# Second pass of an attention and gated linear attention block: halved products, a moved sparse product, a moved carry

## The chip, the cores and the metric

The kernel runs on one core of a Trainium2 chip. The metric is the device time of one execution in microseconds; the median of several executions counts.

## The reference, cut to what matters

The input is two sequences of 4096 tokens with 512 channels. Each goes through a linear attention with 16 heads (first block), and then through gated linear attention with 8 heads of 64 channels (second block). Around each block stand a layer norm, and a residual of another layer norm. The second block, in which the change lies:

```python
q1 = (x @ Wq) * scale; k1 = x @ Wk; v = x @ Wv
q2 = (x @ Wqa @ Wqb) * scale; k2 = softmax(x @ Wka @ Wkb)
gk1 = log_sigmoid(x @ Wg1a @ Wg1b + bg1) / 16
gk2 = log_sigmoid(x @ Wg2a @ Wg2b + bg2) / 16
e = softmax(x @ We); mask = one_hot(top_1(e)); rw = e * mask
o = gla(q1, k1, v, gk1) + sum over the 4 experts of gla(q2 * rw_e, k2 * rw_e, v, gk2 * mask_e)
g = x @ Wga @ Wgb
o = rmsnorm(o) * norm_w * silu(g);  out = o @ Wo
# gla: with G the running sum of gk in a chunk and S the state
#   o_t = (q_t exp(G_t)) S + sum over s <= t of (q_t exp(G_t) . k_s exp(-G_s)) v_s
#   S  <- exp(G_last) S + sum over s of (k_s exp(G_last - G_s)) v_s
```

The first `gla` is called dense here, the four others sparse: a token takes part in one expert alone.

## The kernel before, in words

A first pass over each sequence computes the sums of the linear attention. A second pass goes through the sequence in 32 tiles of 128 tokens, 64 tiles in all, and does the rest for a tile at a time. The change touches the second pass alone.

Five instruction queues run side by side, each in an order written out by hand, and wait for one another on semaphores: TensorE (`pe`), ScalarE (`act`), VectorE (`dve`), GpSimd (`pool`) and SyncE, which loads and stores. Each has a function `step(n, p)`. A step is spread over three tiles: the front of tile n, the back of tile m = n - 1, the tail of tile n - 2, and the first part (`ahead`) of tile n + 1. A queue never takes an instruction before the one that stands ahead of it.

TensorE's step: `low_rank` (the first halves of the low-rank products, bank 7), `route` (the four expert logits, bank 2), `project_v` (bank 1), `gates` (the second halves of gk1, gk2 and g, banks 4 to 6), `label_bc` (spreads each token's expert number over the rows, bank 7), `inter` and `intra` for tile m, then `project_k2`, `project_k`, `den`, `project_q1`, the tail's `og_transpose`, `project_q2`, `cumulate` (running sums of the gates), `out_mm`, `half_sums`, `y_mm`, `transposes`, `state_products`, `scores(n, 0)`, `xn_transpose` of tile n + 1, and `scores(n, 1)`. Matrices of 16 bits go as three products (line 310 to 312); f32 products take two matmul instructions each.

`inter` has two parts. The sparse part (line 481) multiplies the sparse queries with the states of all four experts, in 8 products whose contraction has 64 rows; it fills banks 0 to 3 and signals `ix_pe`. The dense part (line 489) multiplies the dense queries with the dense state, 4 products, into bank 7. `intra` (line 498) adds the scores within the tile times v to bank 7, 8 products.

VectorE's step: the masks of tile m's scores (`back_masks`, `back_carry1`, `back_masks2`), `front_router`, `front_low` (lines 1180 to 1183: the low halves of the low-rank products; `gates` waits for them), `front_label`, `back_carry` (line 1154: the new sparse states are added; the sparse part of `inter` waits for it, as it overwrites their banks), `front_onehot`, `front_masks` (lines 1215 and 1216), `back_select` (lines 1164 and 1167: from banks 0 to 3 each token takes its expert; `project_k2`, line 365, waits for it), `front_prob`, `front_logsig` (line 1222), `back_join`, the softmax of k2, `front_sil`, `back_norm`, qz of tile n + 1, the gated products, `back_normed` (line 1288), `back_gated` (line 1292), `back_out`, `front_decay`, `back_split` (lines 1112 and 1114), `ahead_residual` (line 1121: x1 of tile n + 1) and `ahead_low` (line 1125).

ScalarE's step: `front_low`, `front_label`, `front_v`, then the three passes over the gates (abs, line 729; exp, line 723; ln, line 725; all 1536 columns wide), `front_sig_high` (line 733, behind `front_logsig`), `back_square`, `front_ke`, `front_sig`, `ahead_z`, `back_og` (line 787: copies the transposed output, which `out_mm` needs), `front_exps` (lines 751 to 755), the norms, and the copies of the transposed q and k. The norm of x1 (`ahead_norm2`) is there too; it waits for line 1121. GpSimd adds the two score matrices (line 1018, `back_am`), builds `vm` (line 1025), and computes k2 (lines 1030 and 1034) and the decayed states (lines 1041 and 1042, behind `front_decay`).

Of the kernel before, what the change touches and what calls it, by code (L numbers as in the profile page):

```python
# [5 lines left out]
P = 128  # L28
# [5 lines left out]
H2, D2 = 8, 64  # L34
# [6 lines left out]
HALF = P // 2  # L41
# [24 lines left out]
def sandwich_kernel(nc, x_d, wqkv_d, wproj_d, bproj_d, wb_d, wl_d, ws_d, wo_d, nw_d, consts_d, out_d):  # L66
# [11 lines left out]
    with ExitStack() as ctx:  # L78
# [66 lines left out]
        v, vm = cut(2, C), cut(NEXP, C)  # L145
# [3 lines left out]
        q1T, k1T, q2T, k2T = cut(PAIRS, P), cut(PAIRS, P), cut(PAIRS, P), cut(PAIRS, P)  # L149
        assert cursor[0] <= REGION, cursor  # L150

        am1, am2 = cut(2, PAIRS, P, own=1), cut(2, PAIRS, P, own=1)
        sil, x1 = cut(2, C, own=1), cut(2, C, own=1)
        state0, statex = cut(PAIRS, P, own=1), cut(PAIRS, NEXP * D2, own=1)
# [46 lines left out]
        def S(name):  # L201
            if name not in sems:
                sems[name] = ctx.enter_context(nc.semaphore(name))
            return sems[name]
# [20 lines left out]
        def cur(n):  # L225
            return n + 2

        def prev(n):
            return n + 1
# [72 lines left out]
        def _(pe):  # L302
# [53 lines left out]

            def label_bc(n):
                pe.wait_ge(S("labi_ok"), cur(n))
                pe.wait_ge(S("low_ok"), cur(n))
                mm(bank[7][:, 2 * P:3 * P], ones16[:, :], lab_i[:, :], start=True, stop=True).then_inc(S("rx_pe"), 1)  # L360

            def second(out, which, k):
                if which == 1:
# [4 lines left out]
            def gates(n):  # L368
                pe.wait_ge(S("low_ok"), cur(n))
                pe.wait_ge(S("am1_ok"), prev(n))  # L370
                pe.wait_ge(S("am2_ok"), prev(n))
                for k, which in ((0, 1), (1, 1), (2, 0)):
                    last = second(bank[4 + k], which, k)
                last.then_inc(S("g_pe"), 1)
# [90 lines left out]

            by_row = bank[7].rearrange("p (f o r d) -> p f o r d", f=2, o=2, r=2)

            def inter(n, front):
                pe.wait_ge(S("state_ok"), cur(n))
                pe.wait_ge(S("q2T_ok"), cur(n))  # L470
                pe.wait_ge(S("am1_ok"), cur(n))
                pe.wait_ge(S("carry_ok"), cur(n))
                if front:
                    pe.wait_ge(S("ldiff_ok"), cur(n + 1))
                for half in (1, 0):
                    if half == 0 and front:
                        pe.wait_ge(S("v_ok"), cur(n + 1))
                    for r in range(2):
                        for odd in range(2):
                            h = slice(odd * D2, odd * D2 + D2)  # L480
                            last = mm(psum[:, 2 * half + odd, r * 256:r * 256 + 256], q2T[h, 2 * half + r, :],  # L481
                                      statex[h, 2 * half + r, :], start=True, stop=True)
                last.then_inc(S("ix_pe"), 1)
                if not front:
                    pe.wait_ge(S("out_ok"), n)
                if front:
                    pe.wait_ge(S("same_ok"), cur(n + 1))
                for pr in range(PAIRS):
                    last = mm(by_row[:, pr // 2, :, pr % 2, :], q1T[:, pr, :], state0[:, pr, :].rearrange("p (o d) -> p o d", o=2),
                              start=(pr == 0), stop=False, skip_group_check=True)  # L490
                last.then_inc(S("inter_pe"), 1)

            def intra(n, p):
                pe.wait_ge(S("am_ok"), cur(n))
                for pr in range(PAIRS):
                    for odd in range(2):
                        h = 2 * pr + odd
                        last = mm(by_row[:, pr // 2, odd, pr % 2, :], am1[:, odd, pr, :], v[:, p, h * D2:(h + 1) * D2],
                                  start=False, stop=True, skip_group_check=True)
                last.then_inc(S("o_pe"), 1)  # L500

            def og_transpose(n, back):
# [15 lines left out]
            def step(n, p, front=True, back=True, tail=True, ahead=True):  # L518
                m, mp, t = n - 1, 1 - p, n - 2
                if front:  # L520
                    low_rank(n)
                    route(n)
                    project_v(n)
                    gates(n)
                    label_bc(n)
                if back:
                    inter(m, front)
                    intra(m, mp)
                if front:
                    project_k2(n, back)  # L530
                    project_k(n, back)
                if ahead:
                    den(n + 1, mp, back=back)
                if front:
                    project_q1(n)
                if tail:
                    og_transpose(t, back)
                if front:
                    project_q2(n)
                    cumulate(n, back)  # L540
                if tail:
                    out_mm(t)
                if front:
                    half_sums(n)
                if ahead:
                    y_mm(n + 1)
                if front:
                    transposes(n)
                    state_products(n, p, ahead)
                    scores(n, 0)  # L550
                if ahead:
                    xn_transpose(n + 1, back)
                if front:
                    scores(n, 1)
# [526 lines left out]
        def _(dve):  # L1081
# [92 lines left out]
            def front_low(n):  # L1174
                dve.wait_ge(S("low1_ok"), cur(n))
                up, down = slice(0, LORA), slice(LORA, P)
                g, g_low, g_copy = slice(ROW_G, ROW_ONE), slice(0, 2 * GLR), slice(2 * GLR, 4 * GLR)
                parts = bank[7][:, 0:2 * P].rearrange("p (x c) -> p x c", x=2)
                minus = (ALU.mult, ALU.subtract)
                ve.scalar_tensor_tensor(low[down, 0:4:2, :], parts[up], LOW_SCALE, low[up, 0:4:2, :], *minus)  # L1180
                ve.scalar_tensor_tensor(low[g_low, 1, :], parts[g, 0, :], LOW_SCALE, low[g, 1, :], *minus)
                ve.tensor_scalar(low[g_copy, 1, :], parts[g, 0, :], LOW_SCALE, None, ALU.mult)
                ve.scalar_tensor_tensor(low[up, 3, :], parts[down, 1, :], LOW_SCALE, low[down, 3, :], *minus).then_inc(S("low_ok"), 1)
# [27 lines left out]
            def front_masks(n):  # L1211
                dve.wait_ge(S("rx_pe"), cur(n))
                dve.wait_ge(S("cum_pe"), prev(n))
                row = bank[7][:, 2 * P:3 * P]
                ve.scalar_tensor_tensor(same_d[:, :], row, lab[:, :], centred, ALU.is_equal, ALU.mult)
                ve.scalar_tensor_tensor(same_c[:, :], row, lab[:, :], causal, ALU.is_equal, ALU.mult).then_inc(S("same_ok"), 1)

# [87 lines left out]
            def step(n, p, front=True, back=True, tail=True, ahead=True):  # L1305
                m, mp, t = n - 1, 1 - p, n - 2
                if back:
                    back_masks(m)
                    back_carry1(m)
                    back_masks2(m)  # L1310
                if front:
                    front_router(n)
                    front_low(n)
                    front_label(n)
                if back:
                    back_carry(m)
                if front:
                    front_onehot(n, p)
                    front_masks(n)
                if back:  # L1320
                    back_select(m, mp)
                if front:
                    front_prob(n)
                    front_logsig(n)
                if back:
                    back_join(m)
                if front:
                    front_kmax(n)
                    front_kdiff(n)
                    front_lslow(n)  # L1330
                    front_kfac(n)
                    front_sil(n, p)
                if back:
                    back_norm(m)
                if ahead:
                    ahead_qz(n + 1, mp)
                    ahead_qz_split(n + 1)
                if front:
                    front_gated_1(n)
                    front_gated_q2(n)  # L1340
                if back:
                    back_normed(m)
                    back_gated(m, mp)
                if tail:
                    back_out(t, p)
                if front:
                    front_decay(n, p)
                if back:
                    back_split(m)
                if ahead:  # L1350
                    ahead_residual(n + 1, mp)
                    ahead_low(n + 1, mp)
# [151 lines left out]
```

## Time and profile before

| | |
|---|---|
| median of 3 runs | 2744.33 us (2741.7 to 2745.05) |
| span of the profiled execution | 2739.7 us, 55516 instructions |
| TensorE busy | 2579.3 us, 94% |
| VectorE busy | 1978.2 us, 72% |
| ScalarE busy | 1691.7 us, 62% |
| GpSimd busy | 958.6 us, 35% |

The profiler took one execution, and the page gives its span alone, from its first to its last instruction; no other time stands for that execution. Times in rows count from the start of the span. TensorE's matmuls overlap: where one starts, the one before has not ended, so the distance between two starts tells what a matmul costs in a row of them, and its own duration does not. PEld is TensorE's weight load. Line numbers are those of the kernel before.

### The profile page before, as it was taken

What the parts mean: (1) busy time and instruction counts of PE and PEld (TensorE: products, weight loads), DVE (VectorE), ACT (ScalarE), POOL (GpSimd) and SP (SyncE); (2) the same over time, 40 slices, a digit from 0 to 9 for tenths busy, and PEclk for the clock granted to TensorE, in tenths of its full rate; (3) what the DMA queues carried; (4) which work ended last, traced back from release to release, by engine and by line L of the source; (5) the groups of instructions that cost most, each with busy time, mean ns of one, the idle gap of its engine ahead of it and who ended that gap; (6) DMA issues with size and microseconds to landing.
All of it is one profiled execution on the core that took longest, in us unless ns stands there. A gap on an engine that the chain in (4) does not pass through costs nothing.

```text
span 2739.7 us, 55516 instructions
## 1 busy us (share of the span) xinstructions
PE 2579.3 (94%) x20208; PEld 1612.8 (59%) x20208; DVE 1978.2 (72%) x3750; ACT 1691.7 (62%) x3345; POOL 958.6 (35%) x750
## 2 busy tenths in 40 slices
PE   6999799999999999999869997999999999999997
PEld 3444466666666666666534444666666666666665
DVE  4443388888888888888644423888888888888886
ACT  4433367777777776767433434767677777676774
POOL 2795133333333333333222241333333333333332
PEclk9999899999999999999989998999999999999999
DMA  5121100000000000000022111000000000000000
GB/s 192 62 65 69 39 21 31 23 23 23 23 23 23 27 31 23 23 23 16 24 93 62 61 39 39 28 24 23 23 23 23 23 27 30 23 23 23 23 16 16
DMA packets 48388, 97.65 MB, mean 36 GB/s; under 512 B 5376, under 2 KB 5376, under 8 KB 47680
## 3 DMA queue, kind: packets, MB, share of 16 engines
q1 hardware_dynamic: 37008, 68.44, 7.6%
q10 hardware_dynamic: 9792, 17.83, 1.8%
q0 software_dynamic: 1520, 10.50, 1.0%
q8 instruction: 40, 0.66, 0.1%
q14 instruction: 28, 0.23, 0.0%
HBM read 63.19 MB, written 33.55 MB: 35 GB/s over the span
## 4 chain that ended last, share of the span: by engine, by line
PE 77%; DVE 14%; issue 5%; ACT 3%; DMA 0%; DVEq 0%; ACTq 0%; SPq 0%
PE psum L310 14%; PE psum L312 13%; PE psum L311 13%; PE psum L591 6%; DVE region L1167 5%; PE psum L445 5%; PE psum L481 5%; PE psum L462 4%; PE psum L435 4%; PE psum L321 2%; DVE region L1164 2%; DVE region L1154 2%; PE psum L454 1%; PE psum L365 1%; PE psum L339 1%
## 5 line engine op out<-in xcount | busy, mean ns | idle before, releaser
L310 PE MATMUL psum<-wb,region 128*128 128x512 f16 x768 | 292.0, 380 | 4.9 <-DVE region L1222 4.9
L311 PE MATMUL psum<-wb,region 128*128 128x512 f16 x768 | 292.0, 380 | 0.0
L312 PE MATMUL psum<-wb,region 128*128 128x512 f16 x768 | 291.9, 380 | 0.0
L1018 POOL TENSOR_TENSOR region<-region 128x1024 f32<-128x1024 f32 x64 | 150.2, 2346 | 373.7 <-DVE region L1139 373.7
L1030 POOL TENSOR_TENSOR region<-region,kfac 128x512 f32<-128x512 f32 x64 | 66.8, 1044 | 543.0 <-DVE kfac L1250 543.0
L1013 POOL TENSOR_TENSOR region<-region 128x1024 f32<-128x1024 f32 x64 | 146.5, 2289 | 289.1 <-DVE region L1373 231.1
L1025 POOL TENSOR_SCALAR region<-region,m 128x512 f32<-128x512 f32 x256 | 172.9, 696 | 181.2 <-DVE hm L1203 104.7
L1373 DVE SCALAR_TENSOR_TENSOR region<-psum,region 128x512 f16<-128x512 f32 x64 | 44.3, 692 | 262.2 <-ACT region L850 262.2
L733 ACT ACTIVATE region<-region 128x1024 f16<-128x1024 f32 x64 | 67.6, 1057 | 193.4 <-DVE region L1222 193.4
L591 PE MATMUL psum<-region 128*128 128x512 f16 x768 | 176.2, 379 | 0.0
L481 PE MATMUL psum<-region 64*128 64x256 f32 x1024 | 130.9, 394 | 26.8 <-DVE region L1154 26.8
L1042 POOL TENSOR_TENSOR region<-region,decay 128x1024 f32<-128x1024 f32 x64 | 149.6, 2338 | 0.0
L1034 POOL TENSOR_TENSOR region<-region 128x512 f32<-128x512 f32 x64 | 81.7, 1276 | 192.8 <-ACT region L755 192.8
L1167 DVE SCALAR_TENSOR_TENSOR region<-psum,m,region 128x512 f32<-128x512 f32 x192 | 144.1, 751 | 6.8
L445 PE MATMUL psum<-region 64*128 64x128 f32 x2048 | 148.2, 284 | 0.0
L1125 DVE SCALAR_TENSOR_TENSOR region<-region,rstd 128x512 f16<-128x512 f32 x64 | 48.1, 751 | 138.3 <-ACT region L684 138.3
L445 PEld LDWEIGHTS psum<-region 64*128 64x128 f32 x2048 | 124.1, 187 | 31.1 <-issue 24.6
L850 ACT ACTIVATE region<-psum 128x512 f16<-128x512 f32 x64 | 38.2, 597 | 164.7 <-PE psum L312 164.7
L667 ACT ACTIVATE region<-psum 128x512 f32<-128x512 f32 x256 | 137.5, 589 | 0.0
L481 PEld LDWEIGHTS psum<-region 64*128 64x128 f32 x1024 | 106.2, 190 | 46.2 <-issue 46.0
L1369 DVE TENSOR_TENSOR region<-region 128x512 f16<-128x512 f32 x64 | 95.7, 1496 | 49.8 <-ACT region L863 49.8
L659 ACT ACTIVATE junk<-psum 128x512 f32<-128x512 f32 x128 | 76.6, 599 | 85.9 <-PE psum L312 85.9
(235 smaller groups left out, 7638.4 us busy)
## 6 DMA issues: line engine op xcount, KB each, us to landing
region<-x_in SPq DMA_DIRECT2D x128, 256.0 KB, 2.6
q_cols<-region ACTq DMA_DIRECT2D x64, 256.0 KB, 2.4
region<-q_cols SPq DMA_DIRECT2D x64, 256.0 KB, 2.8
out_rows<-region SPq DMA_DIRECT2D x60, 256.0 KB, 2.0
region<-wb_in POOLq DMA_DIRECT2D x1, 3072.0 KB, 11.6
region<-wqkv_in SPq DMA_DIRECT2D x4, 512.0 KB, 5.8
region<-wqkv_in POOLq DMA_DIRECT2D x2, 1024.0 KB, 5.7
region<-wproj_in POOLq DMA_DIRECT2D x2, 1024.0 KB, 7.5
```

Of the source, the lines that this page charges most:

```text
L310: mm(out, lhs(0), rhs(0), start=start, stop=False)
L311: mm(out, lhs(0), rhs(1), start=False, stop=False)
L312: return mm(out, lhs(1), rhs(0), start=False, stop=stop)
L445: last = mm(bank[where[odd]][:, pr * P:(pr + 1) * P], kT[h, pr, :], qT[h, pr, :], start=True, stop=True)
L481: last = mm(psum[:, 2 * half + odd, r * 256:r * 256 + 256], q2T[h, 2 * half + r, :], statex[h, 2 * half + r, :], start=True, stop=True)
L591: last = mm(bank[4 + j], xn8[:, p * GT + t, x * C + j * P:x * C + (j + 1) * P], k16[:, y_, :], start=first and begins, stop=final and ends ...
L667: ac(dst.rearrange("p a b -> p (a b)"), bank[where], ACT.Copy).then_inc(S(done), 1)
L1013: nc.gpsimd.tensor_tensor(kacc, kacc, k16, ALU.add).then_inc(S("kacc_ok"), 1)
L1018: nc.gpsimd.tensor_tensor(am1[:, :, :, :], am1[:, :, :, :], am2[:, :, :, :], ALU.add).then_inc(S("am_ok"), 1)
L1025: last = nc.gpsimd.tensor_scalar(vm[:, e, :], v[:, p, :], m4[:, p, e:e + 1], 1.0, ALU.mult, ALU.mult)
L1042: nc.gpsimd.tensor_tensor(statex.rearrange("p a (e d) -> p a e d", e=NEXP), carryx.rearrange("p a (e d) -> p a e d", e=NEXP), decay[:, :, ...
L1167: ve.scalar_tensor_tensor(to, of[:, :, e, :], m4[:, p, e:e + 1], to, ALU.mult, ALU.add).then_inc(S("sel_ok"), 1)
```

## The change

Four things are changed. The dense part of `inter` and `intra` are split by output rows: each product of 128 columns of weights becomes two of 64, one for each half of the output's rows. `inter` falls into `inter_sparse` and `inter_dense`; on TensorE, `label_bc` and `inter_sparse` now stand ahead of `gates`, and `inter_dense` and `intra` behind it. The label is spread into bank 6 instead of bank 7, so `label_bc` waits for the masks of tile m (`am2_ok`) and `gates` waits until the label has been read (`same_ok`). On VectorE, `front_label` and `back_carry` stand ahead of `front_low`. 22 empty lines at the top of the file are taken out as well.

```diff
@@ -356,8 +334,8 @@
 
             def label_bc(n):
                 pe.wait_ge(S("labi_ok"), cur(n))
-                pe.wait_ge(S("low_ok"), cur(n))
-                mm(bank[7][:, 2 * P:3 * P], ones16[:, :], lab_i[:, :], start=True, stop=True).then_inc(S("rx_pe"), 1)
+                pe.wait_ge(S("am2_ok"), prev(n))
+                mm(bank[6][:, 0:P], ones16[:, :], lab_i[:, :], start=True, stop=True).then_inc(S("rx_pe"), 1)
 
             def second(out, which, k):
                 if which == 1:
@@ -368,7 +346,7 @@
             def gates(n):
                 pe.wait_ge(S("low_ok"), cur(n))
                 pe.wait_ge(S("am1_ok"), prev(n))
-                pe.wait_ge(S("am2_ok"), prev(n))
+                pe.wait_ge(S("same_ok"), cur(n))
                 for k, which in ((0, 1), (1, 1), (2, 0)):
                     last = second(bank[4 + k], which, k)
                 last.then_inc(S("g_pe"), 1)
@@ -465,7 +443,7 @@
 
             by_row = bank[7].rearrange("p (f o r d) -> p f o r d", f=2, o=2, r=2)
 
-            def inter(n, front):
+            def inter_sparse(n, front):
                 pe.wait_ge(S("state_ok"), cur(n))
                 pe.wait_ge(S("q2T_ok"), cur(n))
                 pe.wait_ge(S("am1_ok"), cur(n))
@@ -481,13 +459,15 @@
                             last = mm(psum[:, 2 * half + odd, r * 256:r * 256 + 256], q2T[h, 2 * half + r, :],
                                       statex[h, 2 * half + r, :], start=True, stop=True)
                 last.then_inc(S("ix_pe"), 1)
+
+            def inter_dense(n, front):
                 if not front:
                     pe.wait_ge(S("out_ok"), n)
-                if front:
-                    pe.wait_ge(S("same_ok"), cur(n + 1))
                 for pr in range(PAIRS):
-                    last = mm(by_row[:, pr // 2, :, pr % 2, :], q1T[:, pr, :], state0[:, pr, :].rearrange("p (o d) -> p o d", o=2),
-                              start=(pr == 0), stop=False, skip_group_check=True)
+                    for rows in (slice(0, HALF), slice(HALF, P)):
+                        last = mm(by_row[rows, pr // 2, :, pr % 2, :], q1T[:, pr, rows],
+                                  state0[:, pr, :].rearrange("p (o d) -> p o d", o=2),
+                                  start=(pr == 0), stop=False, skip_group_check=True)
                 last.then_inc(S("inter_pe"), 1)
 
             def intra(n, p):
@@ -495,8 +475,9 @@
                 for pr in range(PAIRS):
                     for odd in range(2):
                         h = 2 * pr + odd
-                        last = mm(by_row[:, pr // 2, odd, pr % 2, :], am1[:, odd, pr, :], v[:, p, h * D2:(h + 1) * D2],
-                                  start=False, stop=True, skip_group_check=True)
+                        for rows in (slice(0, HALF), slice(HALF, P)):
+                            last = mm(by_row[rows, pr // 2, odd, pr % 2, :], am1[:, odd, pr, rows], v[:, p, h * D2:(h + 1) * D2],
+                                      start=False, stop=True, skip_group_check=True)
                 last.then_inc(S("o_pe"), 1)
 
             def og_transpose(n, back):
@@ -521,10 +502,13 @@
                     low_rank(n)
                     route(n)
                     project_v(n)
+                    label_bc(n)
+                if back:
+                    inter_sparse(m, front)
+                if front:
                     gates(n)
-                    label_bc(n)
-                if back:
-                    inter(m, front)
+                if back:
+                    inter_dense(m, front)
                     intra(m, mp)
                 if front:
                     project_k2(n, back)
@@ -1211,7 +1195,7 @@
             def front_masks(n):
                 dve.wait_ge(S("rx_pe"), cur(n))
                 dve.wait_ge(S("cum_pe"), prev(n))
-                row = bank[7][:, 2 * P:3 * P]
+                row = bank[6][:, 0:P]
                 ve.scalar_tensor_tensor(same_d[:, :], row, lab[:, :], centred, ALU.is_equal, ALU.mult)
                 ve.scalar_tensor_tensor(same_c[:, :], row, lab[:, :], causal, ALU.is_equal, ALU.mult).then_inc(S("same_ok"), 1)
 
@@ -1310,11 +1294,11 @@
                     back_masks2(m)
                 if front:
                     front_router(n)
+                    front_label(n)
+                if back:
+                    back_carry(m)
+                if front:
                     front_low(n)
-                    front_label(n)
-                if back:
-                    back_carry(m)
-                if front:
                     front_onehot(n, p)
                     front_masks(n)
                 if back:
```

## Rows read from the trace of the kernel before

**Rows 1.** The page: busy time, share of the span, instructions of each engine.
```profile
PE 2579.3 (94%) x20208; PEld 1612.8 (59%) x20208; DVE 1978.2 (72%) x3750; ACT 1691.7 (62%) x3345; POOL 958.6 (35%) x750
```

**Rows 2.** Chain in order of time, one step: start us, us, what ran.
```profile
1002.78 0.76 DVE region L1164
...
1005.95 0.39 PE psum L365
...
1034.94 0.76 DVE region L1164
```

**Rows 3.** Waits, 700 to 1300 us: total us, times, longest.
```profile
DVE region L1164 <- PE psum L481: 29.0, 19, 1.6
...
PE psum L365 <- DVE region L1167: 9.2, 19, 0.5
...
PE psum L481 <- DVE region L1154: 5.9, 19, 0.4
...
DVE region L1121 <- ACT rstd L663: 4.5, 19, 0.3
```

**Rows 4.** Timeline, 994 to 1008 us: start, us, engine, line, count [idle before].
```profile
995.05 0.23 PE L310 MATMUL psum<-region,wl 128*128 128x128 f16 x1
...
997.22 0.21 DVE L1191 TENSOR_SCALAR ldiff<-psum,lmax 128x4 f32<-128x4 f32 x1
...
999.08 0.38 PE L312 MATMUL psum<-wb,region 128*128 128x512 f16 x1
...
999.10 1.29 DVE L1154 TENSOR_TENSOR region<-psum,region 128x512 f32<-128x512 f32 x2
...
999.94 0.38 PE L366 MATMUL psum<-ws,region 128*128 128x512 f16 x1
...
1000.36 1.45 ACT L729 ACTIVATE region<-psum 128x1536 f32<-128x1536 f32 x1 [0.23 <-PE psum L366]
...
1000.65 2.00 PE L481 MATMUL psum<-region 64*128 64x256 f32 x16 [0.27 <-DVE region L1154]
...
1000.91 0.34 DVE L1216 SCALAR_TENSOR_TENSOR same_c<-psum,lab,cst 128x128 f32<-128x128 f32 x1
...
1002.57 0.97 PEld L489 LDWEIGHTS psum<-region 128*128 128x128 f32 x8 [0.33 <-issue]
...
1003.40 1.48 ACT L725 ACTIVATE region<-region 128x1536 f32<-128x1536 f32 x1
...
1003.57 1.90 PE L498 MATMUL psum<-region 128*128 128x64 f32 x16
...
1006.11 1.76 DVE L1222 SCALAR_TENSOR_TENSOR region<-psum,region 128x1536 f32<-128x1536 f32 x1
```

**Rows 5.** Timeline, 1011 to 1025 us, of ScalarE, GpSimd, VectorE and TensorE.
```profile
1013.11 1.02 ACT L787 ACTIVATE ogT<-psum 128x1024 f16<-128x1024 f16 x1 [0.97 <-PE psum L509]
...
1016.25 1.27 POOL L1034 TENSOR_TENSOR region<-region 128x512 f32<-128x512 f32 x1 [3.10 <-ACT region L755]
...
1017.19 0.88 DVE L1288 TENSOR_TENSOR og<-region,ors 128x512 f32<-128x512 f32 x1
...
1019.63 1.16 POOL L1041 TENSOR_TENSOR region<-region,decay 128x512 f32<-128x512 f32 x1 [2.10 <-DVE decay L1267]
...
1021.54 0.75 DVE L1121 SCALAR_TENSOR_TENSOR region<-psum,rstd,region 128x512 f32<-128x512 f32 x1 [0.20 <-ACT rstd L663]
...
1021.84 0.69 PE L454 MATMUL psum<-region 128*64 128x64 f32 x16
...
1022.43 1.95 PE L462 MATMUL psum<-region 128*64 128x256 f32 x16
```

**Rows 6.** VectorE's groups by line and shape: total us, mean ns of one.
```profile
L1114 DVE TENSOR_TENSOR og<-og 128x512 f16<-128x512 f32 x64 | 89.4, 1397 | 2.2
...
L1288 DVE TENSOR_TENSOR og<-region,ors 128x512 f32<-128x512 f32 x64 | 55.6, 868 | 1.8 <-ACT ors L782 1.8
...
L1292 DVE TENSOR_TENSOR og<-og,region 128x512 f32<-128x512 f32 x64 | 44.3, 692 | 2.2
```

More of the change, by code:

```diff
@@ L523, in step @@
                     project_v(n)
-                    gates(n)
                     label_bc(n)
                 if back:
-                    inter(m, front)
+                    inter_sparse(m, front)
+                if front:
+                    gates(n)
+                if back:
+                    inter_dense(m, front)
                     intra(m, mp)
@@ L1312, in step @@
                     front_router(n)
-                    front_low(n)
                     front_label(n)
@@ L1317, in step @@
                 if front:
+                    front_low(n)
                     front_onehot(n, p)
```

## The prediction

> **What bounds the kernel now.** I read the page first: TensorE is busy 94% of the span, VectorE 72%, ScalarE 62% [rows 1]. The change touches only the second pass, a loop of 64 tiles. The chain in order of time gives its beat: the same selection instruction starts at 1002.78 and again at 1034.94, so a step lasts 32.16 us [rows 2]. So much for the average; what a moved instruction is worth depends on which queue is late where it stands. The waits between 700 and 1300 us [rows 3] show four, each 19 times in 19 steps: the sparse product L481 waits for the carry L1154 (5.9/19 = 0.31 us a step), the key projection L365 waits for the selection L1167 (0.48), the selection L1164 waits for L481 (1.53), and the residual L1121 waits for rstd (0.24). The reader is to see that TensorE loses about 0.8 us a step around the sparse product, and that VectorE, once the selection has begun, loses only that 0.24 until L1121. VectorE is in front of its work there; it is a second queue with almost no room.
>
> One step in detail [rows 4]. TensorE starts the low-rank product at 995.05, ends the v projection (last start 999.08), does the four gate matmuls (last start 999.94), the label, and at 1000.65 the sparse product. ScalarE takes the gates at 1000.36 (abs), then exp and ln; ln ends at 1003.40 + 1.48 = 1004.88. VectorE's log-sigmoid L1222 needs that ln, but starts only at 1006.11, when the selection is done: ln is 1.23 us early. From 1006.11 VectorE runs its fixed list to L1121, which starts at 1021.54 after an idle 0.20 [rows 5]. L1121 writes x1; from its start to the next low-rank product, one beat after 995.05 at 1027.21, it is 5.67 us of norm, transposes and copy, each waiting for the one before. So a step is a ring: low rank, gates or selection, L1222, VectorE's list, L1121, next low rank.
>
> **The change, part by part, for this step.**
> Carry ahead of the low-rank split: L1191 ends at 997.22 + 0.21 = 997.43; a maximum over four columns and L1154 (1.29) follow, so the carry is there at about 999.0 instead of 999.10 + 1.29 = 1000.39. The four split instructions move behind it; VectorE's list up to L1216 is the same work in another order, so the masks end as before at 1000.91 + 0.34 = 1001.25. The split's reader, the gates, comes after that anyway: no price.
>
> Label and sparse product ahead of the gates: TensorE is free of the v projection 0.22 after 999.08, at 999.30 (from there four matmuls of 512 columns start up to 999.94, 0.215 each). The label has a quarter of the columns, 0.06: 999.36. The carry is no longer waited for. The sparse product uses the array in two row halves; how long such a change of shape takes behind running matmuls stands in no single row. Below: nothing. Above: the weight loader's 0.33 us in front of L489, the change back. I take 0.10, nearer to nothing because the loader's wait lies partly beside the last products. Sparse at 999.46, 1.19 earlier than 1000.65. From L481's start to L489's is 1.92, the change back included: the gates start at 999.46 + 1.92 = 1001.38 (the masks, ended at 1001.25, release the label's bank in time, with 0.13 to spare). The last gate matmul starts 3 x 0.22 later, 1002.03, against 999.94: **the gates are 2.09 us later**.
>
> The Trainium skill (TensorEngine Tiling, Key Properties) says that switching the tiling mode drains the engine. The loader's 0.33 in front of L489 agrees with it; were the first change that long as well, the gates would come 0.23 later than I take, a case inside my range.
>
> Two column halves: 8 dense instructions become 16, and 16 intra-tile ones 32 (each f32 product is two). Intra before: from 1003.57, 16 in 1.90. After, the form is that of L454, 16 of which take 1022.43 - 1021.84 = 0.59 [rows 5], 0.037 each: 32 x 0.037 = 1.18. Dense, 128x64 with 128 columns, is in no row. Below: L454 (64 columns), 0.59. Above: L462 (256 columns), whose 16 are busy 1.95. I take the middle of the spacing by columns, 16 x 0.06 = 1.0, as much as before (1003.57 - 1002.57). So dense and intra end about 1002.03 + 0.22 + 0.1 + 1.0 + 1.18 = 1004.5, between 1004.1 and 1005.5. The selection ends first or last: it begins 2.13 after L481 (1002.78 - 1000.65), and L365 3.17 after that: 999.46 + 2.13 + 3.17 = 1004.76 for L365, against 1005.95. By these numbers TensorE is **1.19 us earlier** at the key projection.
>
> What is late next. ScalarE's abs moves with the gates: 1002.45, and ln ends at 1004.88 + 2.09 = 1006.97. VectorE is done with the selection at 1004.7 and must now wait for ln: L1222 starts at 1007.00, **0.89 later** than before, although everything on TensorE is earlier. Behind L1222 stand the join, the key softmax, the low half of the log-sigmoid, qz, the gated products, the output, the split and L1121, all in VectorE's order, and ScalarE's own list behind L1222's result. TensorE's 1.19 us goes where it meets these: a little at the q projection, which needs L1222, and the rest at the output product, which needs ScalarE's copy L787. That had 0.97 us of idle time in front of it [rows 5], so 0.89 later in its inputs leaves it at about 1013.1, where it was. TensorE is then on the old timetable, and waits again for x1 at L462, which stood right behind L1121's end before (21.54 + 0.75 = 22.29, L462 at 22.43).
>
> VectorE's list, then: +0.89 at L1222; -0.20 because L1121's wait for rstd is used up. One instruction gets shorter: L1288 takes 868 ns on average, L1292 of the same size 692 [rows 6]; L1288 starts at 1017.19 while GpSimd's L1034 runs from 1016.25 for 1.27 [rows 5]. L1034 waits for ScalarE's exponentials, which stand behind L787 and so stay where they were; L1288 comes 0.89 later, when L1034 is over: -0.18. The Trainium skill (SBUF, Who interferes with whom) has the rule: VectorE with two SBUF inputs and GpSimd take one port pair in turns. The rows of L1288 agree. Without that relief the sum would be 62 x 0.69 = 43 us.
>
> Sum: 0.89 - 0.20 - 0.18 = +0.51 us a step. The steps that hold both a tile and the tile before it are 31 a batch, 62 in all: 62 x 0.51 = **32 us**. First and last steps of a batch gain or lose below 1 us each. The profiled execution's span is 2739.7, and the median of the three timed runs 2744.33, 4.6 above; I add the sum to the median: **2776 us**.
>
> Bounds of the likeliest case: no drain and a full relief +0.41, less 0.1 for the rough starts of overlapped rows; a full drain and no relief +0.92. 62 times these: 2763 to 2802. The dense halves' bounds change nothing: up to 1005.5 instead of 1004.76 TensorE is still ahead of where L787 holds it.
>
> **Rivals.**
> (a) *The port pair gives more back (faster).* The split of the gated output, L1114 on og, takes 1397 ns, twice the 692 of L1292 [rows 6], while GpSimd's state product L1041, started at 1019.63 [rows 5], runs beside it. If the shifted list reached L1114 outside L1041, 0.70 us would go, more than the 0.51, and the step would be 0.19 shorter: -12, 2732. It decides once L1114 starts ahead of L1041 instead of behind it. Against it: what releases L1041 is VectorE's decay, just ahead of this split, so the two shift together.
> (b) *VectorE is not held by ln (faster).* If ScalarE's three passes ended early enough, selection and list would both be about 1.1 earlier, 62 x 1.1 = 68, 2676. For it: VectorE waits 1.53 a step for L481 today, and L1222 almost never for ln. Against it: 4.52 us from 1000.36 to 1004.88 are three full-width passes with no idle time to shorten; it turns when ln is less than 0.2 late instead of 0.89.
> (c) *It cancels.* Slack in the ring that the rows don't show (a ScalarE queue behind x1, TensorE at L462) takes most of the 0.51: within 5 us.
> (d) *The halves don't overlap.* At the old intra spacing of 0.11 (16 in 1.9, end included), 48 take 5.3 us; L365 comes at 1007.7, 1.75 later than before, and TensorE, with no wait left, carries it to L462: +108, 2852. Against it: L454's 0.037.
>
> **Chances.** Forecast 0.66, (a) 0.10, (b) 0.10, (c) 0.10, (d) 0.04. A change below 0.2% (5.5 us) can't be told from none. Faster: (a) and (b), 0.20; same: (c), 0.10; slower: the forecast and (d), 0.70. For 8 in 10 the range goes down to 2730, taking in (a), and up to 2805; outside lie (b), (d) and edges. The likeliest alone: 2763 to 2802.
>
> **What would show it.** In the profile after: a beat of about 32.7; L481 at some 4.4 us after the low-rank start instead of 5.6; VectorE's wait for L481 nearly gone, and in its place some 2 us a step in front of L1222, released by the ln L725; TensorE waiting for L787 at the output product and for L1121 at L462; L498's successors at 0.037 each; L1288 at 0.69. If L1222 shows no wait for ln, or the beat is under 32.1, the prediction is wrong; if the wait is there and the beat is not longer, VectorE's list had room that I did not see.

## The result and the profile after

The changed kernel takes 2772.12 us, median of 4 runs (2771.02 to 2773.53), against 2743.28 for the kernel before in the same rounds: a ratio of 1.0106, with a 95% interval of 1.0091 to 1.0120. It is 28.8 us slower; forecast were 2776 us, with a range of 2730 to 2805, and slower with a chance of 0.70. Its profiled execution has a span of 2770.1 us, 30.4 more than before.

Line numbers move by the deleted empty lines and the new ones. L1222 is now L1206, L1121 is L1105, L1288 is L1272, L1114 is L1098, L725 is L709, L787 is L771, L481 is L459, L365 is L343, L1164 is L1148, L462 is L440, L1112 is L1096, L1125 is L1109, and GpSimd's L1041 and L1042 are L1025 and L1026.

The chain of waits of the changed kernel in order of time, without the many matmuls of the projections (start us, us, what ran). It answers to [rows 2].

```profile
1007.38 0.23 PE psum L288
...
1011.84 1.93 PE psum L459 x16
1013.77 0.54 PE psum L342 x2
...
1014.77 1.46 ACT region L713
1016.23 0.18 ACT lexp L702 x2
1016.41 1.38 ACT region L707
1017.81 1.49 ACT region L709
...
1034.28 0.75 DVE region L1105
1035.03 0.14 issue
1035.17 1.95 PE psum L440 x16
...
1039.88 0.23 PE psum L288
```

This is the ring of the prediction in one piece: low rank, sparse product, gates, ScalarE's three passes, VectorE's list, x1, TensorE, next low rank. A turn is 1039.88 - 1007.38 = 32.50 us, against 32.16. The page's summary of the whole chain says the same: the first line is of the kernel before, the second of the changed kernel. TensorE's share falls from 77% to 51%, VectorE's and ScalarE's grow.

```profile
PE 77%; DVE 14%; issue 5%; ACT 3%; DMA 0%; DVEq 0%; ACTq 0%; SPq 0%
PE 51%; DVE 27%; ACT 12%; issue 9%; DVEq 0%; DMA 0%; SPq 0%; ACTq 0%
```

The same step in the timeline (start, us, engine, line, count, idle time before and what ended it), beside [rows 4, 5].

```profile
1011.77 2.00 PE L459 MATMUL psum<-region 64*128 64x256 f32 x16
...
1013.91 0.75 DVE L1148 TENSOR_SCALAR region<-psum,m 128x512 f32<-128x512 f32 x1 [0.44 <-PE psum L459]
...
1014.36 0.38 PE L344 MATMUL psum<-ws,region 128*128 128x512 f16 x1
...
1014.66 1.09 PE L468 MATMUL psum<-region 128*64 128x128 f32 x16
...
1015.59 1.10 PE L479 MATMUL psum<-region 128*64 128x64 f32 x32
...
1017.08 0.39 PE L343 MATMUL psum<-ws,region 128*128 128x512 f16 x1 [0.39 <-DVE region L1151]
...
1019.33 1.76 DVE L1206 SCALAR_TENSOR_TENSOR region<-psum,region 128x1536 f32<-128x1536 f32 x1 [2.05 <-ACT region L709]
```

Count from the low-rank start, 995.05 before and 1007.38 after. The sparse product comes at 4.39 instead of 5.60, the key projection L343 at 9.70 instead of 10.90. The gates' last matmul comes at 6.98 instead of 4.89, and L1206 at 11.95 instead of 11.06, after 2.05 us in which VectorE does nothing. TensorE is 1.2 us early, and gives it back further on, where it waits for ScalarE's copy and for x1:

```profile
1026.34 0.39 PE L288 MATMUL psum<-wo,ogT 128*128 128x512 f16 x1 [0.69 <-ACT ogT L771]
```

The waits between 700 and 1300 us (total, times, longest), answering to [rows 3]. VectorE's wait for the sparse product is down from 29.0 to 7.9, its wait for ln, which had no row before, is 36.8, and TensorE has two new ones.

```profile
DVE region L1206 <- ACT region L709: 36.8, 18, 2.0
...
PE psum L288 <- ACT ogT L771: 13.1, 19, 0.7
...
PE psum L440 <- DVE region L1105: 9.4, 19, 0.5
...
DVE region L1148 <- PE psum L459: 7.9, 18, 0.4
...
PE psum L343 <- DVE region L1151: 7.0, 18, 0.4
```

Where the 30.4 us are, by the starts of the selection L1148. Its 29 middle distances of a sequence are 32.50 instead of 32.16 or 32.17: 2 x 29 x 0.335 = 19.4. The first distance of each sequence is 34.86 and 34.84 instead of 31.05: 7.6. The last is 1.2 and 1.4 longer: 2.6. The first selection comes 1.1 later, which need not be the change's: over the eleven profiles of this case it lies anywhere between 358.8 and 363.9. Together 30.7; the way from the first sequence to the second and the end of the second make up the rest.

### The profile page after: what moved, and what is told of

Read it like the earlier page. It is cut to its first block, busy times and chain, and to the rows that moved or that the text cites. A ratio compares the mean times of both kernels' runs of the same rounds, so it can differ in the third digit from the quotient of the medians.

```text
span 2770.1 us, 58588 instructions
## 1 busy us (share of the span) xinstructions
PE 2557.9 (92%) x21744; PEld 1544.3 (56%) x21744; DVE 1965.7 (71%) x3750; ACT 1689.6 (61%) x3345; POOL 970.1 (35%) x750
## 4 chain that ended last, share of the span: by engine, by line
PE 51%; DVE 27%; ACT 12%; issue 9%; DVEq 0%; DMA 0%; SPq 0%; ACTq 0%
PE psum L288 9%; PE psum L289 8%; PE psum L290 8%; PE psum L575 6%; PE psum L423 5%; PE psum L459 5%; PE psum L440 4%; ACT region L709 3%; ACT region L713 3%; ACT region L707 3%; DVE region L1215 2%; DVE region L1256 2%; DVE region L1105 2%; DVE region L1287 2%; DVE region L1156 2%
## 5 line engine op out<-in xcount | busy, mean ns | idle before, releaser
L1002 POOL TENSOR_TENSOR region<-region 128x1024 f32<-128x1024 f32 x64 | 150.8, 2356 | 358.8 <-DVE region L1123 358.8
L1206 DVE SCALAR_TENSOR_TENSOR region<-psum,region 128x1536 f32<-128x1536 f32 x64 | 112.5, 1757 | 131.9 <-ACT region L709 131.9
L713 ACT ACTIVATE region<-psum 128x1536 f32<-128x1536 f32 x64 | 93.1, 1455 | 148.5 <-PE psum L344 148.5
L440 PE MATMUL psum<-region 128*64 128x256 f32 x1024 | 124.5, 383 | 28.9 <-DVE region L1105 28.9
L1026 POOL TENSOR_TENSOR region<-region,decay 128x1024 f32<-128x1024 f32 x64 | 149.5, 2336 | 0.0
L1109 DVE SCALAR_TENSOR_TENSOR region<-region,rstd 128x512 f16<-128x512 f32 x64 | 48.0, 751 | 134.9 <-ACT region L668 134.9
L423 PEld LDWEIGHTS psum<-region 64*128 64x128 f32 x2048 | 124.1, 187 | 31.0 <-issue 24.6
L288 PE MATMUL psum<-wo,ogT 128*128 128x512 f16 x256 | 99.7, 389 | 44.5 <-ACT ogT L771 44.5
L459 PE MATMUL psum<-region 64*128 64x256 f32 x1024 | 131.4, 397 | 7.7 <-DVE region L1138 7.7
```

Source lines behind the costliest of these rows:

```text
L288: mm(out, lhs(0), rhs(0), start=start, stop=False)
L423: last = mm(bank[where[odd]][:, pr * P:(pr + 1) * P], kT[h, pr, :], qT[h, pr, :], start=True, stop=True)
L440: last = mm(psum[odd * D2:odd * D2 + D2, 3 * (pr // 2), (pr % 2) * 256:(pr % 2) * 256 + 256], k2g[:, h * D2:(h + 1) * D2], vm[:, :, h * D2 ...
L713: ac(gch, psum[:, 4:7, :].rearrange("p a b -> p (a b)"), ACT.Abs).then_inc(S("abs_ok"), 1)
L1002: nc.gpsimd.tensor_tensor(am1[:, :, :, :], am1[:, :, :, :], am2[:, :, :, :], ALU.add).then_inc(S("am_ok"), 1)
L1026: nc.gpsimd.tensor_tensor(statex.rearrange("p a (e d) -> p a e d", e=NEXP), carryx.rearrange("p a (e d) -> p a e d", e=NEXP), decay[:, :, ...
```

## The experiments

The theory is that of the prediction. The rivals are that TensorE's new order or array shapes cost the time, and that time saved on TensorE counts wherever it is saved. The ratios are to runs of the kernel before in the same rounds.

**The halves alone**, on the kernel before:

```diff
-  last = mm(by_row[:, pr // 2, odd, pr % 2, :], am1[:, odd, pr, :], v[...], ...)
+  for rows in (slice(0, HALF), slice(HALF, P)):
+      last = mm(by_row[rows, pr // 2, odd, pr % 2, :], am1[:, odd, pr, rows], v[...], ...)
   (the dense product likewise; every order as before)
```

> The kernel before with the column halves alone; every order as before. Theory (the step is a ring through VectorE's list, and ScalarE's gate passes decide when L1222 starts): the dense and intra-tile products get about 0.7 us shorter, and the key projection behind them still waits for the selection; the beat stays 32.16 and the time 2743, within 3. Rival 1 (the halves or their change of array shape cost the time): slower, near 2772. Rival 2 (TensorE's time counts wherever it is saved): 62 x 0.7 = 43 less, 2700.

Measured: 2742.14 us, ratio 0.9998 (0.9988 to 1.0007): no change. The waits (same columns) show where the saved time went; in [rows 3] the key projection's line has 9.2.

```profile
DVE region L1167 <- PE psum L481: 29.0, 19, 1.5
...
PE psum L365 <- DVE region L1170: 25.7, 19, 1.4
```

The key projection now waits 1.35 us a step for the selection instead of 0.48. The 0.87 that dense and intra-tile products save turns into that wait, and the beat stays 32.16. The halves are cheap, and here worth nothing.

**The order alone**, the changed kernel with the two products whole again:

```diff
-  for rows in (slice(0, HALF), slice(HALF, P)):
-      last = mm(by_row[rows, ...], am1[:, odd, pr, rows], v[...], ...)
+  last = mm(by_row[:, ...], am1[:, odd, pr, :], v[...], ...)
   (the dense product likewise)
```

> The changed kernel with the column halves undone; the new orders stay. Theory: dense and intra-tile products take about 0.7 us more, the key projection comes about 0.4 later, and TensorE then only waits less for ScalarE's copy at the output product: the beat stays 32.50, the time 2772, within 4. Rival 1 (the halves cost the time): back near 2743. Rival 2 (TensorE decides): 2772 + 62 x 0.4 = 2797 or more.

Measured: 2773.88 us, ratio 1.0113 (1.0097 to 1.0130), a beat of 32.50. All of the loss is in the new order. L343's wait is gone from the waits, and the log-sigmoid's (L1203 here) is the same 36.8 as with the halves. One part of the expectation missed: TensorE's wait for the copy does not shrink, it stays at 13.0 in 19 steps.

**The late gates alone.** This puts the forecast cause into the kernel before without touching TensorE or VectorE:

```diff
   act.wait_ge(S("g_pe"), cur(n))
   act.wait_ge(S("ls_ok"), prev(n))
+  ac(gch, psum[:, 4:7, :]..., ACT.Copy).then_inc(S("pad_ok"), 1)
+  act.wait_ge(S("pad_ok"), n * 2 + 1)
+  ac(gch[:, 0:C], bank[4], ACT.Copy).then_inc(S("pad_ok"), 1)
+  act.wait_ge(S("pad_ok"), n * 2 + 2)
   ac(gch, psum[:, 4:7, :]..., ACT.Abs).then_inc(S("abs_ok"), 1)
```

> The kernel before with two idle passes (1536 and 512 columns, about 2.1 us) put on ScalarE ahead of the gates' abs: nothing moves on TensorE or VectorE, the gates only come as late to L1222 as in the changed kernel. Theory: ln ends 2.1 later, 0.87 behind the selection; less the 0.2 of slack and 0.2 to 0.3 of relief the beat is 32.4 to 32.6, the time 2758 to 2775. Rival (the loss comes from TensorE's new order or shapes, not from the late gates): 2743, as ScalarE is busy only 62%.

Measured: 2769.41 us, ratio 1.0095 (1.0079 to 1.0112). The beat alternates around 32.52. Two microseconds on an engine that is busy 62% of the span bring back 26 of the 29 us. In its profile the middle distances, 0.35 a step longer, make 20.2, against 19.4 in the changed kernel; the first distances are 31.98 and 33.07 instead of 34.86 and 34.84, so the loss at the edges is not the same one.

```profile
DVE region L1226 <- ACT region L725: 15.2, 18, 0.9
```

L1226 is the log-sigmoid here; it waits 0.84 a step for ln, the amount by which ln passed the selection.

**A shorter ln** in the changed kernel. It leaves out the logarithm of the gates but for one column:

```diff
-  ac(gch, gch, ACT.Ln, bias=1.0).then_inc(S("ln_ok"), 1)
+  ac(gch[:, 0:1], gch[:, 0:1], ACT.Ln, bias=1.0).then_inc(S("ln_ok"), 1)
```

> The changed kernel with the third gate pass (ln) done on one column instead of 1536, so the gates are left without their logarithm; about 1.3 us less on ScalarE ahead of L1222. Theory: L1222 comes 1.3 earlier and VectorE's list with it; the beat falls from 32.50 to 31.2 to 31.5, below that of the kernel before, since TensorE's earlier order then arrives: 2690 to 2712. Rival (TensorE's order or the halves cost the time): 2772, unchanged.

Measured: 2686.54 us, ratio 0.9795 (0.9779 to 0.9811).

```profile
L709 ACT ACTIVATE region<-region 128x1 f32<-128x1 f32 x64 | 13.0, 203 | 2.0
```

The instruction takes 203 ns instead of 1484, 1.28 us less, and the beat is 31.22 instead of 32.50: the ring gets shorter by what ScalarE's pass does, one for one. With it the kernel takes 56 us less than the kernel before. What the shorter ln would do there was not run; in [rows 4] ln ends 1.23 us before it is needed.

**The wait filled.** Nothing is left out; VectorE does in the idle 2.05 us what came later, and ScalarE's order follows.

```diff
   (VectorE, behind back_select)
-  front_prob, front_logsig, back_join, front_kmax, front_kdiff, front_lslow, front_kfac, front_sil
+  back_join, front_prob, front_kmax, front_kdiff, front_logsig, front_kfac, front_lslow, front_sil
   (ScalarE, behind front_gates(n, 1))
-  front_sig_high, back_square, front_ke, front_sig
+  back_square, front_ke, front_sig_high, front_sig
```

> The changed kernel with work put where VectorE waits for ln: the join, the factors of the key softmax, its maximum and difference stand ahead of L1206, the sums behind it ahead of the low half; on ScalarE the square and the key exponential stand ahead of the 16-bit copy of the log-sigmoid. Nothing is left out. Theory (VectorE's list behind ln is the ring): about 1.9 of the 2.05 us of waiting fill, until TensorE's own sum stands in the way, 32.16 - 0.31 - 0.48 - 0.72 = 30.7: a beat of 30.7 to 31.3, 2655 to 2690. Rival (the loss comes from TensorE's order or shapes): 2772, or above.

Measured: 2680.52 us, ratio 0.9776 (0.9760 to 0.9793), a beat of 31.1. The groups by line (total us, mean ns, idle before) of the changed kernel and then of this one:

```profile
L1206 DVE SCALAR_TENSOR_TENSOR region<-psum,region 128x1536 f32<-128x1536 f32 x64 | 112.5, 1757 | 131.9 <-ACT region L709 131.9
```

```profile
L1206 DVE SCALAR_TENSOR_TENSOR region<-psum,region 128x1536 f32<-128x1536 f32 x64 | 112.5, 1758 | 2.5 <-ACT region L709 2.4
```

131.9 us of idle time have become 2.5, and the time is 92 us below the changed kernel. 1.4 of the 2.05 us a step arrive. Then TensorE has one wait left, 0.39 a step for the selection, as in the changed kernel; the rest of the 31.09 is its own work. The same filling of the kernel before was not run.

**The filled wait without the halves**, the same edit as in the second experiment:

> The same with the column halves undone. Theory: with VectorE's wait filled TensorE is the bound, and its 0.7 us in dense and intra-tile products now count: 25 to 45 above the kernel with the filled wait. Rival (VectorE's list still decides, as in the changed kernel): within 4 of it.

Measured: 2700.33 us (2696.07 to 2704.62), ratio 0.9840 (0.9823 to 0.9857), 19.8 above the kernel with them: less than expected. The profile below is of an execution of 2704.62. The beat is 31.42 instead of 31.09, 0.33 a step where the first experiment had the halves save 0.87 on TensorE. With the halves, L343 waits for the selection:

```profile
PE psum L343 <- DVE region L1151: 7.8, 20, 0.4
```

Without them that wait has no row. Counted from the gates' last matmul, L343 starts at 2.83 us (1021.59 to 1024.42) instead of 2.73 (1012.74 to 1015.47): without its wait of 0.39 the way is 0.49 shorter with the halves, and only 0.10 of that is left behind the wait. It is less than 0.87 because without a wait L343 starts 0.17 before the recorded end of L476 (1022.69 + 1.90), from which waits are counted, and because the halves' first product starts 0.31 behind the last gate matmul, the whole one 0.21, and the whole one is short here, 0.89 instead of 1.00. The larger part comes through VectorE. The join (L1153 here) was moved ahead of the log-sigmoid (L1203) to fill the wait, and it needs the intra-tile product L476:

```profile
DVE region L1153 <- PE psum L476: 8.7, 19, 0.5
PE psum L288 <- DVE region L1203: 4.0, 19, 0.2
```

The chain has them in this order:

```profile
1022.86 1.75 PE psum L476 x16
1024.71 0.69 DVE region L1153
...
1026.90 1.76 DVE region L1203
1028.71 0.39 PE psum L288
```

The log-sigmoid starts 5.76 us behind the selection's start instead of 5.42, and TensorE waits 0.21 a step for it at the q projection. So the halves are worth something once VectorE's wait is gone, and not before, but mostly because the join no longer waits for the intra-tile product, not because TensorE's own work is shorter.

**The split ahead of the decay**, in the changed kernel, for rival (a):

```diff
-  front_decay(n, p), back_split(m)
+  back_split(m), front_decay(n, p)
```

> The changed kernel with VectorE's decay moved behind the split of the gated output, so that GpSimd's state products no longer run beside the split. Theory (one of the two engines holds the shared port for a whole instruction): the split falls from 1.42 to 0.69 and x1 comes 0.65 earlier, but the state products start 1.1 later and now stand in front of L1109, which reads two operands from SBUF: L1109 waits or runs 0.6 to 0.9 longer, the beat is 32.4 to 32.7, the time 2768 to 2785. Rival (the split is long for another reason, or L1109 can run beside GpSimd): 0.65 less a step, 2732.

Measured: 2738.09 us, ratio 0.9981 (0.9972 to 0.9991), a beat of 31.91. The expectation was half wrong: the split did what it says, but the time is near the rival's 2732 and far below 2768. VectorE's and GpSimd's groups with both instructions of the split and the state products, of this kernel:

```profile
L1109 DVE SCALAR_TENSOR_TENSOR region<-region,rstd 128x512 f16<-128x512 f32 x64 | 48.1, 751 | 138.2 <-ACT region L668 138.2
...
L1098 DVE TENSOR_TENSOR og<-og 128x512 f16<-128x512 f32 x64 | 44.3, 692 | 2.2
```

```profile
L1026 POOL TENSOR_TENSOR region<-region,decay 128x1024 f32<-128x1024 f32 x64 | 121.9, 1905 | 0.0
...
L1025 POOL TENSOR_TENSOR region<-region,decay 128x512 f32<-128x512 f32 x64 | 67.1, 1048 | 246.2 <-DVE decay L1251 245.9
```

The split falls from 1396 to 692 ns, as expected. But the state products get shorter as well (L1026 from 2336 to 1905, L1025 from 1162 to 1048), so they are over at 1025.45 + 1.91 = 1027.36, just as L1109 starts at 1027.33, and L1109 keeps its 751 ns.

```profile
1025.45 1.91 POOL L1026 TENSOR_TENSOR region<-region,decay 128x1024 f32<-128x1024 f32 x1
...
1027.33 0.75 DVE L1109 SCALAR_TENSOR_TENSOR region<-region,rstd 128x512 f16<-128x512 f32 x1 [2.16 <-ACT region L668]
```

I had left out that the collision had cost GpSimd time too. The Trainium skill (SBUF, Who interferes with whom) calls the port an exclusive lock. The trace agrees roughly: in the changed kernel the split and the two products together fill 1032.65 to 1036.12, 3.47 us, and their times alone add up to 0.69 + 1.05 + 1.91 = 3.65, as if nearly one after the other.

**Both together:**

> The kernel with the filled wait, and the decay moved behind the split of the gated output as well. Theory: in the filled kernel TensorE and VectorE are about level (undoing the halves cost 0.35 a step of the 0.7 that they are worth on TensorE), so of the 0.6 us that the split's free port gave the changed kernel only a part arrives: 0.1 to 0.4 a step, 2655 to 2675. Rival 1 (VectorE's list alone is the bound): 0.6 a step, 2643. Rival 2 (TensorE alone): 2680, unchanged.

Measured: 2677.74 us, ratio 0.9760 (0.9744 to 0.9776), the lowest median here, though its interval overlaps the filled kernel's. The beat of 31.08 is that of the filled kernel; rival 2 is right. The 0.7 us that the split saves stands in front of x1, where VectorE's wait grows from 4.5 in 19 steps (0.24 each) to 0.97 each:

```profile
DVE region L1105 <- issue: 18.4, 19, 1.0
```

The two profiled spans are 2.4 us apart; the first distances (30.07 and 30.09, now 29.49 both) and the last ones bring 2.2 of it. With intervals that overlap, that is no more than a hint.

**TensorE kept at work in the second step**, for the part of the loss that the prediction had not seen. Ahead of its qz product (L304), in that step alone:

```diff
+  if ahead and back and not tail:
+      pe.wait_ge(S("osum_ok"), cur(m))
+      for g in range(KT):
+          mm3(bank[7], lambda x: xnT[:, x, g, :], lambda x: wb[:, x, g, 0:C], g == 0, g == KT - 1)
   if ahead:
       y_mm(n + 1)
```

In the changed kernel, TensorE's timeline there and the table of stretches (busy us of each engine and instructions, granted clock, DMA):

```profile
377.45 0.61 PE L304 MATMUL psum<-bias,ones 128*128 128x512 f16 x1 [2.78 <-DVE region L1098]
377.85 0.63 PE L288 MATMUL psum<-mix,region 128*128 128x512 f16 x1
378.28 0.63 PE L289 MATMUL psum<-mix,region 128*128 128x512 f16 x1
```

```profile
360.00:374.00 14.00, 12.69 (x106) 7.11 (x103) 11.17 (x21) 9.41 (x15) 3.66 (x5) 1.00 0.01 1
374.50:377.40 2.90, 0.18 (x7) 0.08 (x4) 2.83 (x6) 2.36 (x8) 1.26 (x1) 0.72 0.00 0
377.40:382.80 5.40, 5.35 (x13) 1.99 (x14) 5.02 (x8) 0.00 (x0) 2.06 (x2) 0.52 0.01 3
```

> The changed kernel with twelve matmuls whose result is not used, in the second step of each sequence alone, where TensorE waits 2.78 us for qz ahead of its bias product and then runs that product with a granted clock of 0.52. Theory (the idle time lets the clock fall, and that is 2.8 of the 3.8 us that this step is longer than in the kernel before): the clock stays at 1.00, the step goes from 34.85 to about 32.1, twice: the span 5.6 less, 2766 to 2768. Rival (the step is long for VectorE's list alone, and TensorE's product is hidden): 2772, unchanged.

Measured: 2769.48 us, ratio 1.0092 (1.0078 to 1.0105). The same product, with the twelve matmuls in front of it:

```profile
378.59 0.39 PE L304 MATMUL psum<-bias,ones 128*128 128x512 f16 x1 [0.17 <-DVE region L1102]
378.81 0.38 PE L288 MATMUL psum<-mix,region 128*128 128x512 f16 x1
379.03 0.38 PE L289 MATMUL psum<-mix,region 128*128 128x512 f16 x1
```

```profile
377.40:382.80 5.40, 5.23 (x31) 3.01 (x30) 5.30 (x10) 1.78 (x5) 1.04 (x2) 1.00 0.00 0
```

The clock stays at 1.00, and the matmuls start 0.22 apart instead of 0.43. The step is 32.91 instead of 34.86: 1.95 of its excess of 3.8 goes with the clock. I had expected 2.8; of the 0.85 that is missing, 0.50 is a wait of TensorE for x1 at L440, which it does not have in this step of the changed kernel. Two steps save 3.9 us, the medians differ by 2.6, and the two intervals of the ratio overlap: the clock and the distance show the effect, the total time hardly. It lies between the 2766 to 2768 expected and the rival's 2772.

## Why the prediction was right

Point by point, by its own steps, counted from the low-rank start.

- *The sparse product 1.19 earlier*: 5.60 to 4.39, 1.21. The change of shape took 0.15 from the label's start (1011.62 to 1011.77), of which I had 0.16.
- *The gates 2.09 later*: 4.89 to 6.98, exactly that.
- *L1222 0.89 later*: 11.06 to 11.95, exactly that, with the 2.05 us of idle VectorE in front of it that the prediction named as its sign.
- *The key projection 1.19 earlier*: 10.90 to 9.70. Dense halves 0.058 each (forecast 0.06), intra halves 0.034 (forecast 0.037).
- *TensorE loses it again at the output product*: there, 0.69, and at L440, 0.5.
- *L1288 shorter by 0.18*: 868 to 689 ns.
- *VectorE's list to x1*: +0.41, forecast +0.51. The mis-sized term is the slack ahead of L1121. I read 0.20 from its wait; but without a wait L1105 starts 0.08 before the recorded end of the split ahead of it (1034.28 against 1032.94 + 1.42), so the slack was 0.29.
- *The beat*: +0.34, forecast +0.51. Besides that 0.1, 0.07 is the ring's last part, which I took as 5.67, from a mean beat of 32.16. Before, the turns from low rank to low rank alternate between 32.09 and 32.24, and the step that I read is a short one; from x1 to the next low rank it is 5.60 in either kernel.
- *Edge steps below 1 us each*: wrong. Four of them brought 10.2 us, a third of the loss. The prediction gave no reason for this bound. In the second step there is no output product for TensorE to wait at; it runs on to the qz product and waits there 2.78 us for VectorE's late list, and the clock falls. The same list meets GpSimd there: L1096, 0.43 in a full step, takes 1.46. The last distances, 2.6 of the 10.2, I did not take apart; part of them may be the clock and not the list. In both kernels the granted clock falls inside them (0.94 before, 0.91 after), and in the kernel with the order alone the longer of the two has the lower clock (us, busy us of each engine and instructions, granted clock, DMA):

```profile
1338.50:1367.10 28.60, 23.97 (x193) 16.03 (x192) 20.76 (x34) 14.57 (x26) 9.86 (x8) 0.91 0.15 47
2718.20:2745.68 27.48, 22.85 (x193) 15.23 (x192) 20.79 (x34) 14.56 (x26) 9.93 (x8) 0.97 0.03 11
```

So 62 steps x 0.51 = 32 came out as 19.4 in the middle and 10.2 at the edges: the total of 2772 against 2776 is closer than its parts. That the total comes so near is luck, two misses that cancel; the sign, and the beat that the middle steps share, are right by the ring and not by that luck: the experiments with the late gates alone and with the shorter ln change nothing but ScalarE's chain, and the beat follows.

Rival (a) did not happen: the split kept its 1396 ns. But its price was near: with the decay moved behind the split, 0.59 a step comes back, of the 0.70 that (a) names. Rival (b)'s condition, ln in time, is what the filled kernel makes, in another way than (b) had it, and its time of 2676 is near the 2680.5 measured there. Rivals (c) and (d) are ruled out by the beat and by the halves' 0.034.

## What to carry to other kernels

A product moved ahead of another on an in-order engine moves the other one back by its own length, and the price is set by whoever consumes that other one: follow its result through each engine to the point where it meets a queue without slack. Saved time on the busiest engine (94%) was worth nothing while a ring through two less busy engines was as long as its own; a wait of 2 us in front of a fixed list is worth filling before anything else is shortened. Price the first and last steps of a loop by their own waits, since what hides a delay in a full step may be missing there.

## What the runs showed of the hardware

Weights of 64 columns in f32 cost TensorE 0.034 us an instruction for 64 moving columns (L479, 32 in 1.10) and 0.058 for 128 (L468, 16 in 0.93), in pairs that fill the two column halves; with 128 columns of weights the 64-column product took 1.90 / 16 = 0.12. After 2.78 us in which TensorE stood idle, the granted clock was 0.52 over the next 5.4 us, near the 1.2 GHz level, and the matmuls there started 0.43 apart instead of 0.22; idle pieces of 0.4 to 0.7 us in the full steps left it at 1.00. A collision of VectorE and GpSimd over SBUF cost both: 0.70 us on the split and 0.55 on the two state products (1396 ns against 692, and 2336 + 1162 against 1905 + 1048).
